# Cross attention's scores as three float32r products of split queries and keys, with keys in a ring of two quads

## The reference, cut to what matters

```python
q = (query @ Wq.T + bq).reshape(b, lq, HEADS, HEAD_DIM)
k = (key @ Wk.T + bk).reshape(b, lk, HEADS, HEAD_DIM)
v = (value @ Wv.T + bv).reshape(b, lk, HEADS, HEAD_DIM)
scores = jnp.einsum('bqhd,bkhd->bhqk', q * scale, k)
probs = jax.nn.softmax(scores, axis=-1)
attn = jnp.einsum('bhqk,bkhd->bqhd', probs, v).reshape(b, lq, HIDDEN)
```

## Time and profile before

| | |
|---|---|
| runs | 2391.12, 2385.10, 2385.49 us; median 2385.49 |
| profiled execution | 2388.18 us, its span 2386.4 us |
| TensorE busy | 2329.8 us (98% of the span), granted clock 0.994 |
| VectorE, ScalarE, GpSimd busy | 1509.9, 1347.0, 1401.0 us |
| DMA | 384.6 MB, mean 161 GB/s |

### The profile page before, as it was taken

The page is one execution under the profiler, slowest core; times in us unless marked ns, Lnnn a source line. Parts: engine busy times, 40 slices in busy tenths (PEclk is TensorE's granted clock), DMA queues, the critical chain, the costliest instruction groups (busy, mean ns, idle before and its releaser), DMA issues.

```text
span 2386.4 us, 58682 instructions
## 1 busy us (share of the span) xinstructions
PE 2329.8 (98%) x21642; PEld 2032.3 (85%) x21642; DVE 1509.9 (63%) x2563; ACT 1347.0 (56%) x3322; POOL 1401.0 (59%) x1211
## 2 busy tenths in 40 slices
PE   8999989999999999999999999999999899999999
PEld 7888858988888888888888888888887699998998
DVE  4666788836767677676767677676776734435342
ACT  5878852236666666666666666666665652221321
POOL 4777677357667667666666667667664533333332
PEclk9999979999999999999999999999999999999999
DMA  7444478537777777777777777777677841101010
GB/s 190 130 130 115 123 207 323 205 99 199 189 195 199 201 196 192 197 204 201 185 200 197 197 198 196 197 199 198 188 189 192 248 133 38 49 18 66 6 34 24
DMA packets 254793, 384.60 MB, mean 161 GB/s; under 512 B 116728, under 2 KB 132152, under 8 KB 254520
## 3 DMA queue, kind: packets, MB, share of 16 engines
q1 hardware_dynamic: 229944, 330.65, 49.3%
q10 hardware_dynamic: 24576, 50.36, 8.2%
HBM read 126.33 MB, written 40.60 MB: 70 GB/s over the span
## 4 chain that ended last, share of the span: by engine, by line
PE 74%; DVE 1%; issue 1%; ACT 1%; ACTq 0%; DMA 0%; SPq 0%; POOL 0%; DVEq 0%; POOLq 0%
PE D_ps_p L69 41%; PE D_ps_s L1978 7%; PE E_ps_g L69 6%; PE E_ps_u L69 6%; PE D_ps_p L2005 6%; PE E_ps_d L69 5%; PE E_ps_y L69 3%; ACT D_e L1633 1%; DVE D_columns L1775 1%; ACTq L1649 0%; DMA D_pT<-D_turned 0%; PE E_ps_t L2034 0%; DVE D_turned L1789 0%; SPq L1371 0%; ACT D_values L1622 0%
## 5 line engine op out<-in xcount | busy, mean ns | idle before, releaser
L1494 POOL TENSOR_SCALAR D_e<-D_e,D_columns 128x722 f32<-128x722 f32 x256 | 539.4, 2107 | 440.7 <-DVE D_columns L1781 440.6
L1775 DVE TENSOR_REDUCE D_columns<-D_ps_s 128x1 f32<-128x723 f32 x512 | 439.4, 899 | 346.2 <-PE D_ps_s L1978 346.0
L1633 ACT ACTIVATE D_e<-D_ps_s,D_columns 128x723 f32<-128x723 f32 x512 | 437.3, 862 | 232.9 <-DVE D_columns L1775 232.7
L1789 DVE STREAM_TRANSPOSE D_turned<-D_e 128x768 f32<-128x768 f32 x512 | 495.3, 972 | 27.4 <-DMA D_pT<-D_turned 26.8
L69 PE MATMUL D_ps_p<-D_ctx_high,cross_wk_high 128*128 128x384 f32 (+1 forms) x1024 | 346.2, 338 | 4.3 <-ACT D_values L1622 2.3
L69 PE MATMUL D_ps_p<-D_ctx_low,cross_wk_high 128*128 128x384 f32 (+1 forms) x1024 | 333.4, 326 | 0.0
L69 PE MATMUL D_ps_p<-D_ctx_high,cross_wk_low 128*128 128x384 f32 (+1 forms) x1024 | 333.2, 325 | 0.0
L1640 ACT ACTIVATE D_e<-D_e,D_columns 128x722 f32<-128x722 f32 x256 | 230.4, 900 | 65.7 <-DVE D_columns L1781 65.7
L69 PE MATMUL D_ps_p<-cross_wv_high,D_ctx_low 128*128 128x512 f32 (+1 forms) x656 | 257.6, 393 | 0.0
L69 PE MATMUL D_ps_p<-cross_wv_low,D_ctx_high 128*128 128x512 f32 (+1 forms) x656 | 257.4, 392 | 0.0
L69 PE MATMUL D_ps_p<-cross_wv_high,D_ctx_high 128*128 128x512 f32 (+1 forms) x656 | 255.6, 390 | 0.9 <-ACT D_values L1622 0.9
(11 more groups left out here) (264 smaller groups left out, 5220.0 us busy)
## 6 DMA issues: line engine op xcount, KB each, us to landing
D_pT<-D_turned SPq DMA_DIRECT2D x1536, 96.0 KB, 2.6
D_pT<-D_turned ACTq DMA_DIRECT2D x512, 96.0 KB, 2.8
D_craw<-in_ctxT SPq DMA_DIRECT2D x124, 361.0 KB, 4.2
self_v<-wstage SPq DMA_DIRECT2D x25, 256.0 KB, 2.6
A_v<-self_v SPq DMA_DIRECT2D x32, 200.0 KB
self_o<-A_o SPq DMA_DIRECT2D x32, 200.0 KB, 3.8
x<-C_x SPq DMA_DIRECT2D x5, 1280.0 KB, 5.8
cross_q<-C_qo SPq DMA_DIRECT2D x20, 320.0 KB, 3.9
```

The costliest lines, as they stand in the source:

```text
L1494: pool.tensor_scalar(head, head, inv[:, 2 * (s % 2):2 * (s % 2) + 1], None, ALU.mult)\
L1633: act.activation(e[n // 2 % 2][:, n % 2, 0:PARTS * PART].rearrange("p (a c) -> p a c", a=PARTS), parts_of(n), ACT.Exp, bias=neg_max[:, n % ...
L1775: dve.tensor_reduce(neg_max[:, n % 4:n % 4 + 1], parts_of(n), AX.XY, ALU.max, negate=True)\
L1789: dve.transpose(turned[quad % 2][:, :, 2 * (s % 2) + h, :].rearrange("p j (t r) -> p t j r", r=32), e[s % 2][:, h, :].rearrange("p (t j r) ...
```

## The change

Queries and keys of cross attention are now split into a high and a low part (float32r), and the scores are three products of them: 36 matmuls per quad, accumulated in PSUM, in three parts of 242 columns, where there were 12 float32 ones of 241. GpSimd makes the low queries with a subtract, VectorE the low keys with one instruction per key unit out of PSUM; a key unit's bank is free only when the low keys are made (`k_low`). Keys and queries are kept for two quads and not for four, and key units are made in the pair ahead of their scores. Context pieces and tails are split at other steps, queries are loaded per quad. `load_first_outputs` and the output weights' load are cut in halves and moved in SyncE's order. In self-attention ScalarE takes the unit of slot 1 ahead of the exponentials of that slot. `TAIL`, `FIRST` and the names of some semaphores change with it. The rest of the diff is waits on renamed semaphores and their counts.

```diff
@@ -692,10 +692,14 @@
                             high_o(1, 1)
                         if b > 0 and i == 1:
                             take_result(b - 1)
+                        if i == 1:
+                            for u in slot(s, 1):
+                                take_unit(u)
                         if 0 <= c < B and i < 2:
                             exps(c, i)
-                        for u in slot(s, i):
-                            take_unit(u)
+                        if i != 1:
+                            for u in slot(s, i):
+                                take_unit(u)
                     if s in WO_STEP:
                         act.wait_ge(next_loaded, 64)
...
-    PART = -(-S // PARTS)
+    PART = -(-S // (2 * PARTS)) * 2
+    KEYS_AHEAD = 2
+    QUERIES_AHEAD = 3
...
     THIRD = 32
     STEPS = PAIRS * B
     SUM_AFTER = 6
     V_STEP = (5, 6, 7, 9, 10, 11)
-    QUERY_STEP = (2, 4, 6, 7)
-    PIECE_STEP = (4, 5, 7, 8)
-    FIRST = -6
+    PIECE_STEP = (6, 7, 10, 11)
+    FIRST = -4
     MAIN = STEPS - 4
-    TAIL = MAIN // 2 - 3
+    TAIL = MAIN // 2 - 2
     SLOTS = 4
+    USED_ONCE = 16
     RESULT_AT = {1: QUADS * B - 2, 5: QUADS * B - 1}
     TURNED_FREE = {5: QUADS * B - 2, 16: QUADS * B - 1}
...
-        ks = rest("D_keys", [P, QUADS, S])
+        both_keys = rest("D_keys", [P, 4, S], F32R)
+        ks = [both_keys[:, 2 * part:2 * part + 2, :] for part in range(2)]
         qraw = rest("D_qraw", [P, QUADS, T])
-        qs = rest("D_queries", [P, QUADS, BLOCKS, 32])
+        qs = Split(rest, "D_queries", [P, 2, BLOCKS, 32])
...
-                unit_at.setdefault(PAIRS * (b - 1) + u + 2, []).append(("k", b, u))
+                unit_at.setdefault(PAIRS * b + u - KEYS_AHEAD, []).append(("k", b, u))
             for i in range(ST - is_fourth(b)):
                 step = FOURTH_V_STEP[i] if is_fourth(b) else V_STEP[i]
                 unit_at.setdefault(PAIRS * (b - 1) + step, []).append(("v", b, i))
             for m in range(QUADS):
                 sum_at[PAIRS * b + 2 * m + SUM_AFTER] = QUADS * b + m
-                queries_at[PAIRS * (b - 1) + QUERY_STEP[m]] = (b, m)
+                queries_at[2 * (QUADS * b + m) - QUERIES_AHEAD] = QUADS * b + m
             for k in range(KD):
                 if b > 0:
                     piece_at.setdefault(PAIRS * (b - 2) + PIECE_STEP[k], []).append((b, k))
...
         def wait_bank(pe, *item):
 
             if item[0] == "o" and item[1] >= TAIL:
-                pe.wait_ge(k_done, KU * B)
+                pe.wait_ge(k_low, KU * B)
                 pe.wait_ge(v_done, values_taken(B))
                 pe.wait_ge(o_done, item[1])
                 return
...
-                def load_q(b):
-                    wait(sp, q_done, QUADS * b)
-                    sp.dma_start(qraw[:, :, :], q_rows[:, :, col(b * T, T)]).then_inc(q_loaded, 16)
+                def load_q(quad):
+                    b, m = quad // QUADS, quad % QUADS
+                    if b < B:
+                        wait(sp, q_low, quad - QUADS + 1)
+                        sp.dma_start(qraw[:, m, :], q_rows[:, m, col(b * T, T)]).then_inc(q_loaded[m], 16)
 
                 def store(b):
                     sp.wait_ge(o_done, QUADS * (b + 1))
...
-                def load_first_outputs():
-                    sp.wait_ge(u_done, max(unit_count[i] for i in unit_count if i[1] == B - 2))
-                    sp.wait_ge(c_low, KD * B)
-                    sp.dma_start(wo_raw[:, :, :], wo.rearrange("(k p) n -> p k n", p=P)).then_inc(wo_loaded, 16)
-                    for par in range(2):
-                        sp.wait_ge(stored[par], 16 * (GT * 2 // T // 2 + 1))
-                    sp.dma_start(acts_raw[:, :, :], eo_rows[:, :, 0:GT]).then_inc(o_loaded, 16)
+                def load_wo(half):
+                    if half == 0:
+                        sp.wait_ge(c_low, KD * B)
+                    chunks = slice(half * KD // 2, (half + 1) * KD // 2)
+                    sp.dma_start(wo_raw[:, chunks, :], wo.rearrange("(k p) n -> p k n", p=P)[:, chunks, :])\
+                      .then_inc(wo_loaded[half], 16)
+
+                def load_first_outputs(half):
+                    if half == 0:
+                        sp.wait_ge(u_done, max(unit_count[i] for i in unit_count if i[1] == B - 2))
+                        for par in range(2):
+                            sp.wait_ge(stored[par], 16 * (GT * 2 // T // 2 + 1))
+                    chunks = slice(half * KD // 2, (half + 1) * KD // 2)
+                    sp.dma_start(acts_raw[:, chunks, :], eo_rows[:, chunks, 0:GT]).then_inc(first_loaded[half], 16)
 
                 def load_weights(n):
...
                 load_ctx(1, 3)
                 sp.wait_ge(t_clear, 1)
                 load_tails(0, 0)
                 load_tails(0, 1)
+                load_q(QUADS)
+                load_q(QUADS + 1)
                 for b in range(B - 1):
-                    load_q(b + 1)
                     if b > 0:
                         move(QUADS * b - 1)
+                        load_q(QUADS * b + 5)
+                        load_ctx(b + 1, 3)
+                    if b % 4 == 1 and b // 4 < FOURS:
+                        load_tails(b // 4, 2)
+                    move(QUADS * b)
+                    load_q(QUADS * b + 6)
                     if b + 2 < B:
                         load_ctx(b + 2, 0)
                         load_ctx(b + 2, 1)
-                    move(QUADS * b)
                     if b % 4 == 1 and b // 4 < FOURS:
-                        load_tails(b // 4, 2)
+                        load_tails(b // 4, 3)
                     if b > 0:
                         store(b - 1)
                     if b + 2 == B:
-                        load_first_outputs()
+                        load_wo(0)
                     if b % 4 == 3 and (b + 1) // 4 < FOURS:
                         load_tails((b + 1) // 4, 0)
                         load_tails((b + 1) // 4, 1)
                     move(QUADS * b + 1)
-                    if b % 4 == 1 and b // 4 < FOURS:
-                        load_tails(b // 4, 3)
+                    load_q(QUADS * b + 7)
+                    if b + 2 == B:
+                        load_wo(1)
+                        load_first_outputs(0)
+                    move(QUADS * b + 2)
+                    load_q(QUADS * b + 8)
                     if b + 2 < B:
                         load_ctx(b + 2, 2)
-                        load_ctx(b + 2, 3)
-                    move(QUADS * b + 2)
+                    if b + 2 == B:
+                        load_first_outputs(1)
 
                 last = QUADS * B - 1
                 move(last - 4)
...
-                def block_queries(b, m):
-                    pool.wait_ge(q_loaded, 16 * (b + 1))
-                    wait(pool, s_done, QUADS * (b - 1) + m + 1)
-                    pool.tensor_copy(qs[:, m, :, 0:QB], qraw[:, m, :].rearrange("p (a q) -> p a q", a=BLOCKS))\
-                        .then_inc(q_done, 1)
+                def block_queries(quad):
+                    b, m = quad // QUADS, quad % QUADS
+                    pool.wait_ge(q_loaded[m], USED_ONCE + 16 * (b + 1))
+                    wait(pool, s_done, quad - 1)
+                    raw = qraw[:, m, :].rearrange("p (a q) -> p a q", a=BLOCKS)
+                    high, low = (qs[part][:, quad % 2, :, 0:QB] for part in range(2))
+                    pool.tensor_copy(high, raw).then_inc(q_high, 1)
+                    pool.wait_ge(q_high, quad + 1)
+                    pool.tensor_tensor(low, raw, high.bitcast(F32), ALU.subtract).then_inc(q_low, 1)
 
                 def split_piece(b, k):
                     if k == 0:
...
-                    wait(act, s_done, QUADS * (b - 1) + m + 1)
-                    act.activation(ks[:, m, first:end], bank("k", b, u)[:, 0:end - first], ACT.Identity,
-                                   bias=bk_c[:, m:m + 1]).then_inc(k_done, 1)
+                    wait(act, s_done, QUADS * b + m - 1)
+                    act.activation(ks[0][:, m % 2, first:end], bank("k", b, u)[:, 0:end - first], ACT.Identity,
+                                   bias=bk_c[:, m:m + 1]).then_inc(k_high, 1)
 
                 def take_values(b, i):
                     rows = P if i < ST - 1 else LAST
...
                 dve.wait_ge(b_loaded, 32)
-                dve.wait_ge(consts, 8)
+                dve.wait_ge(consts, 9)
                 dve.wait_ge(all_max, 2)
                 dve.tensor_scalar(inexact[:, :], biggest_all[:, :], EXACT, None, ALU.is_gt).then_inc(flagged, 1)
+
+                def low_keys(s):
+                    for kind, b, u in unit_at.get(s, []):
+                        if kind == "k":
+                            m, (first, end) = u // 2, HALVES[u % 2]
+                            dve.wait_ge(k_high, KU * b + u + 1)
+                            dve.scalar_tensor_tensor(ks[1][:, m % 2, first:end], bank("k", b, u)[:, 0:end - first],
```

(47 more changed lines are left out.)

49 lines of the change are left out of this document (27 added, 22 removed).

## The result

The changed kernel takes 2408.02 us (median of 4 runs, 2404.63 to 2409.71) beside 2387.04 for the kernel before on the same chip: ratio 1.0084, 95% interval 1.0072 to 1.0096. It is slower by 21 us, where 8 us less was predicted. The profiled execution took 2409.71 us, its span is 2407.9. Of the executions of all kernels in this document one, of the run best, took 5188.68 us where its other four took 2365.10 to 2370.35; the ratios leave it out, and no run shows what it was.

What follows compares the result with a forecast made beforehand. TensorE was taken to bound the steady part (busy 1272.5 of 1274.8 us). Steady part +3, self-attention -8, start -3 and end 0 summed to -8 us, so 2377.5 us was predicted, own range 2368 to 2387, wider range 2357 to 2402.

Steps and rivals of the forecast that it cites:

- Scores on TensorE: Cross attention's score blocks: nine float32r rounds of 0.111 us replace six float32 rounds, saving about 0.16 us per quad.
- the 0.07 for part 2: In each scores block, 0.07 us charged because the third part must wait for the first to leave a shared bank.
- Rival C: Scores: float32r rounds aren't cheap in this tile shape, so the kernel ends slower, 2475 or about 2700 us; chance 0.15.
- The low keys on VectorE: Steady part: two instructions of 0.56 and 0.51 us delay the maxima; short periods +9 us, long ones -8.
- I charge 1.5 us in all: Steady part, long periods behind short ones: cost of ScalarE taking the last values about 0.4 us late.
- uses up nearly all the slack of the bank: Steady part: the values' take, about 0.4 us late, nearly exhausts the slack of the bank the next keys want.
- Self-attention, -8: Self-attention: taking the second unit ahead of eight exponentials ends TensorE's waits for A_q and A_k; bounds -9 and -1.
- if nothing else there is as long: Condition on self-attention's -8 us: no other chain there is as long; VectorE and ScalarE wait on each other too.
- The start, -3: Start of cross attention: fewer key units precede the first scores, which come near 507.4 and not 510.52: -3 us.
- The end, 0 give or take 3: Last quads: one period shortens by 5.8 us, the next two grow by 1.8 and 3.9.
- Rival B: Softmax chain longer than forecast (late values' take or VectorE, +13), or self-attention gives gain back (+7): 2384 to 2398; chance 0.25.

Runs made afterwards that it cites:

- best: The changed kernel with the edits of values_ahead, own_maximum and end_again together: 2365.87 us, ratio 0.9905.
- no_low_keys: The changed kernel without VectorE's low keys, the third product of the scores reading the high keys again: 2371.21 us, one run.
- own_maximum: The changed kernel with each exponential waiting for its own maximum, not both of its step, heads reordered: 2396.81 us, ratio 1.0029.
- values_ahead: The changed kernel with ScalarE's take of a pair's last values ahead of the two DMA issues of the diagonal moves: 2391.94 us, ratio 1.0025.
- end_again: values_ahead with the end spread as in values_end, but the last two high outputs made after step 250: 2390.41 us, ratio 1.0007.
- values_end: values_ahead with the high and low parts of output weights and outputs at the end made at other steps: 2395.24 us, ratio 1.0023.
- control: The changed kernel as it is, profiled and timed a second time: 2407.94 us, ratio 1.0071.

## Why the prediction was wrong, by its own steps

- **Scores on TensorE.** Right. Rounds of 0.11, a block of 1.24 us (1.28 said). The saving is 0.20 and not 0.16, so the 0.07 for part 2 was about twice too much. Rival C, which had 0.15, is out.
- **The low keys on VectorE.** Right: 0.62 and 0.56 us recorded (0.56 and 0.51 said), maxima at 5.99, short periods of 9.66 (9.64 said) and long ones of 12.07. +10 and -8 us, as forecast (the prediction counted 66 short periods, there are 67). no_low_keys and own_maximum show that it is these two instructions ahead of the maxima.
- **"I charge 1.5 us in all" for ScalarE's late take of the last values.** This is the step that failed. I had seen that it "uses up nearly all the slack of the bank", and then priced the regular case. The slack was cover for something irregular, DMA issues of 1.4 to 2.3 us in place of 0.5 to 0.6, which the trace of before had too, with 2.3 us of waits to show for it. It measured 13 us: TensorE waits 13.5 us for those takes in the changed kernel and 0.7 in values_ahead, where 15.4 of the steady part come back.
- **Self-attention, -8.** Failed too: about -1 (1.4 less, give or take 2). I had written that it holds "if nothing else there is as long" and didn't look for what is: the weighted sums, for which TensorE waits 3.4 us in place of none. That they are late because the edit makes the exponentials later is argued and not shown.
- **The start, -3.** Right (18.2 us from the first unit to the first scores where it was 21.0). Not in the sum was that quads 0 to 4 are held by the softmax chain too: +1.4.
- **The end, 0 give or take 3.** Quad 126 took 15.15 (15.0 said). Quad 124 took 10.3 to 10.9 and not 9.64, since, by ScalarE's order of time, two conversions of the output weights (1.15 us at 1860.49) stand ahead of a take of keys; no run tests that. Quad 125 took 17.9 and 16.3 in the two profiles and not 12.06: VectorE's subtracts ran into GpSimd's, and the take of the last values came late here too. In all +7.4 and +5.4.

Rival B named the late take of the values and the self-attention that gives its gain back, but its ceiling (13 us for the steady part, 7 for self-attention) ended at 2398. The misses in the steady part and at the end are of one kind: cover that was there was taken as free.

## What to carry to other kernels

Before an edit eats slack, look in the trace of before for what that slack has been absorbing: the longest instance of an instruction, not its median, is what the cover must hold. A take that frees a bank for the bound engine should stand ahead of DMA issues in its queue, since those can be held up by things that the program doesn't contain. When two mended faults are worth more together than apart (own_maximum alone 11 us, behind values_ahead 22), the first was hiding the second.

## What was not expected of the hardware

- A DMA issue on ScalarE can be held until a fetch of instructions is through, 1.09 to 2.33 us in place of 0.51 to 0.61: 18 of 18 and 5 of 5 issues over 1.0 us overlap a 16 KB packet, though only 18 of 33 and 5 of 33 that overlap one are held. In end_again and values_end one issue each, of 1.7 and 1.9 us, overlaps a packet of 8 KB of that kind in its place. The fetches' place in the loop follows from the length of TensorE's program and comes back from run to run (quads 43 to 68 in the profile, 43 to 67 in control).
- Twelve waits on a long past semaphore, of which the trace records six, cost TensorE 0.24 to 0.3 us per quad.
- VectorE's subtract of two operands in SBUF (128x512) takes 1.73 to 2.06 us beside GpSimd's subtract, and mostly 0.67 to 0.69 beside GpSimd's scaling by a column.
- GpSimd pays 5.6 to 5.8 us ahead of the all-reduce and 6.9 to 7.6 ahead of the first subtract behind it, be it of queries or of context.
